# One transformer block on one core: the second sequence's value units moved up, and the shared opening in a new order

## The reference

```
xn = layernorm(x)
q, k, v, o = xn @ Wq.T, xn @ Wk.T, xn @ Wv.T, xn @ Wog.T
i, f = 15*tanh((xn @ Wig.T + big)/15), 15*tanh((xn @ Wfg.T + bfg)/15)
for each token t, each head:
    m' = max(logsigmoid(f) + m, i);  F = exp(logsigmoid(f) + m - m');  I = exp(i - m')
    C = F*C + I*k v^T;  n = F*n + I*k;  m = m'
    h = (q/sqrt(32)) C / (max(|q/sqrt(32) . n|, exp(-m)) + 1e-6)
x = x + (sigmoid(o) * gamma * headnorm(h)) @ Wout.T
w_q = sign(w) * (|w| >= 0.7 * mean|w|)            for w1 (2048x512) and w2 (512x2048)
x = x + gelu(layernorm(x) @ w1_q.T + b1) @ w2_q.T + b2
```

## Time and profile before

| | |
|---|---|
| median of three runs | 1740.55 us |
| the profiled execution, whole | 1742.3 us |
| its span (first to last instruction) | 1740.6 us |
| mean granted TensorE clock | 0.996 |
| busy: VectorE, ScalarE, POOL | 83%, 61%, 35% |
| instructions | 31380 |
| moved by DMA | 187.45 MB, mean 108 GB/s |

### The profile page before, as it was taken

One profiled execution on the slowest core, in us unless ns is written; L12 is line 12 of the kernel. 1 busy time (PEld: TensorE's weight loads), 2 busy tenths in 40 slices (PEclk: granted clock), 3 DMA queues, 4 the chain that ended last, 5 costly groups with the idle time before them and its releaser, 6 DMA issues.

```text
span 1740.6 us, 31380 instructions
## 1 busy us (share of the span) xinstructions
PE 1707.5 (98%) x12028; PEld 841.4 (48%) x12028; DVE 1437.6 (83%) x2528; ACT 1059.6 (61%) x1769; POOL 606.6 (35%) x477
## 2 busy tenths in 40 slices
PE   6899999999999999999999999999999999999999
PEld 4554445444444444445444444444444444454455
DVE  7888788897888978789887888988789788886872
ACT  6978375473746638375573746648375573847643
POOL 1242514335241442514235241442514235241430
PEclk9999999999999999999999999999999999999999
DMA  8736253442725326253442725336262442625120
GB/s 321 219 89 167 58 141 72 117 120 56 170 60 127 87 80 160 58 154 59 120 117 56 171 60 126 87 92 152 55 161 61 110 119 56 148 59 132 33 55 25
DMA packets 294981, 187.45 MB, mean 108 GB/s; under 512 B 239136, under 2 KB 260640, under 8 KB 289712
## 3 DMA queue, kind: packets, MB, share of 16 engines
q1 hardware_dynamic: 293248, 182.30, 41.7%
q10 hardware_dynamic: 1584, 3.15, 0.5%
HBM read 96.47 MB, written 20.23 MB: 67 GB/s over the span
## 4 chain that ended last, share of the span: by engine, by line
PE 81%; DVE 8%; DMA 3%; SPq 3%; issue 2%; POOL 1%; ACT 1%; POOLq 0%; DVEq 0%; ACTq 0%
PE pf L2073 24%; PE pf L2057 22%; PE pa L1926 17%; PE pa L1902 7%; PE psh L1926 5%; SPq L530 2%; PE psh L2013 2%; DMA kT<-shared 1%; PE psh L1968 1%; PE psh L2047 1%; DVE gT L1633 1%; PE pa L2013 1%; DVE dec L1482 1%; PE pa L1893 1%; PE psh L2009 1%
## 5 line engine op out<-in xcount | busy, mean ns | idle before, releaser
L2073 PE MATMUL pf<-w2T,gT 128*128 128x512 f16 x2048 | 505.8, 379 | 0.0
L2057 PE MATMUL pf<-x2T,w1T 128*128 128x512 f16 x1920 | 422.0, 379 | 0.0
L2057 PEld LDWEIGHTS pf<-x2T,w1T 128*128 128x128 f16 x1920 | 185.4, 98 | 222.5
L2073 PEld LDWEIGHTS pf<-w2T,gT 128*128 128x128 f16 x2048 | 195.5, 97 | 177.0
L1633 DVE SCALAR_TENSOR_TENSOR gT<-g,wscale,gT 128x512 f16<-128x512 f32 x240 | 208.5, 871 | 22.5 <-ACT gT L1046 20.2
L1926 PE MATMUL pa<-wT,xT 128*128 128x512 f16 x960 | 212.8, 379 | 0.6 <-ACT sig L970 0.6
L1043 ACT ACTIVATE g<-pf,b1c 128x512 f32<-128x512 f32 x240 | 164.1, 684 | 72.5 <-PE pf L2057 56.6
L1046 ACT ACTIVATE gT<-g,wscale 128x512 f16<-128x512 f32 x240 | 173.3, 722 | 7.9
L1926 PE MATMUL pa<-wT,shared 128*128 128x512 f16 x768 | 176.2, 379 | 1.6 <-DMA shared<-qT 0.8
L1051 ACT ACTIVATE ktok<-kT 128x512 f32<-128x512 f32 x64 | 40.4, 631 | 216.4 <-DVE kT L1528 214.9
L1902 PE MATMUL pa<-xT,wT 128*128 128x512 f16 x768 | 171.4, 379 | 0.0
(11 more groups left out here) (246 smaller groups left out, 2705.2 us busy)
## 6 DMA issues: line engine op xcount, KB each, us to landing
dec<-gate_r SPq DMA_DIRECT2D x32, 1024.0 KB, 6.1
xin<-L_attn_x SPq DMA_DIRECT2D x16, 1024.0 KB, 6.0
out<-x1b SPq DMA_DIRECT2D x64, 256.0 KB, 2.3
xres<-L_attn_x SPq DMA_DIRECT2D x16, 512.0 KB, 4.3
xres<-L_attn_x SPq DMA_DIRECT2D x32, 256.0 KB, 3.0
qw<-gate_w SPq DMA_DIRECT2D x128, 48.0 KB, 2.0
s<-state_w SPq DMA_DIRECT2D x60, 97.5 KB, 2.4
qw<-kT SPq DMA_DIRECT2D x120, 48.0 KB, 2.0
```

The source lines that it names most:

```text
L2057: last = nc.tensor.matmul(bank, w1T[:, k, tok(f)], x2T[:, part, :, k, :], start=(k == 0 and part == HI), stop=(k == KD - 1 and part == LO))
L2073: last = nc.tensor.matmul(bank, gT[:, part, f, tok(t)], w2T[:, f, :], start=(f == 0 and part == HI), stop=(f == NF - 1 and part == LO), sk ...
```

## The change

What moves, by engine:

- TensorE: the transpose of the row maxima and their sum are two functions, with x's transposes or weight transposes between them. gates(0), which put four slices of k side by side on column quarters, is first_gates, which sums all twelve matmuls on one set of 32 rows. scores(0, 1) stands ahead of the ternary transposes 2 to 4. Of the 18 filler matmuls ahead of ternary transpose 10, five stay; value unit 1 of sequence 1 follows them, in the bank pf[:, 1]. Value units 2 and 3 of sequence 1 stand ahead of project(0, 2).
- VectorE: no sum of gate quarters in sequence 0, and its gate logarithms stand in the setup; the high half of x(1) and the absolute sums of a quarter of w1 (absolute_sums) stand ahead of chunk_decay; the low half of x(1) stands between weigh(3) and weigh(4). The halves lie in xres and no longer in g32 and qT.
- ScalarE: the first function is a square of a small constant; tanh of sequence 0 reads the product directly; the sums of w1 and w2 are in another order, with two of w1 gone; squares of chunks 0 and 1 come ahead of a small2_gone each; value unit 1 of sequence 1 is copied out in the middle of the ternary work.
- POOL: in sequence 0 the masks wait for the decays' exponentials (d_ok), and weigh waits for the masks.
- SP: the order is the same; the load of xres for sequence 0 also waits for x(1)'s transposes.

The core of the diff:

```diff
-        x1_halves = [part[:, :, :].bitcast(F16).rearrange("p g s -> p (g s)").rearrange("p (t d) -> p t d", d=D) for part in (g32, qT)]
+        x1_halves = [part[:, :, :].bitcast(F16).rearrange("p g s -> p (g s)").rearrange("p (t d) -> p t d", d=D) for part in (xres[:, 0:T // 2, :], xres[:, T // 2:T, :])]
...
+                    sp.wait_ge(x1T_loaded, 32)
...
             def earlier_only(b, n):
-                for h in (2 * n, 2 * n + 1):
-                    if in_ps(h):
-                        pool.wait_ge(ps_free[h % 2], ps_done(b, h))
-                    else:
-                        pool.wait_ge(pa_free[h % 2], pa_done(b, score_use(h)))
+                if isinstance(b, int) and b == 0:
+                    pool.wait_ge(d_ok, 2 * n + 2)
+                else:
+                    for h in (2 * n, 2 * n + 1):
+                        if in_ps(h):
+                            pool.wait_ge(ps_free[h % 2], ps_done(b, h))
+                        else:
+                            pool.wait_ge(pa_free[h % 2], pa_done(b, score_use(h)))
...
-                value(b, 1)
+                if not (isinstance(b, int) and b == 1):
+                    value(b, 1)
...
+            def first_exponents():
+                bank = pa_bank(0, U_GATE)
+                act.wait_ge(pa_fill, pa_filled(0, U_GATE))
+                nc.scalar.activation(th, pa[0:GROWS, bank, :], ACT.Tanh, bias=gate_bias[:, 0:1],
+                                     scale=evac[0:GROWS, W_GATE:W_GATE + 1]).then_inc(tanh_ok, 1)
+                act.wait_ge(tanh_ok, 1)
+                nc.scalar.activation(ge, th[0:NH, :], ACT.Abs).then_inc(pa_free[bank], 1)
+                act.wait_ge(pa_free[bank], pa_done(0, U_GATE))
+                nc.scalar.activation(ge, ge, ACT.Exp, scale=-CAP).then_inc(gate_act, 1)
             def opening():
-                gate_copy(0)
-                absolute_sums2(1, 2)
-                gate_tanh(0)
+                absolute_sums2(0)
+                first_exponents()
+                absolute_sums2(1)
                 value(0, 0)
-                gate_exp(0)
-                absolute_sums1(6, early=True)
+                gate_log(0)
                 weights_hi(*USES_QK[0:3])
                 value(0, 1)
                 weights_hi(USES_QK[3])
-                gate_log(0)
+                replace_rows(G_QK)
+                absolute_sums1(6, early=True)
                 value(0, 2)
-                replace_rows(G_QK)
                 weights_hi(*USES_O[0:2])
+                gate_floor(0)
                 value(0, 3)
-                gate_floor(0)
                 act.wait_ge(s_abs, sums.n)
                 keys(0, 0)
                 late_decays(0)
                 weights_hi(USES_O[2])
                 keys(0, 1)
-                absolute_sums2(3)
                 weights_hi(USES_O[3])
+                absolute_sums2(2)
                 replace_rows(G_O)
                 queries(0, 0)
                 gate_columns(0)
-                absolute_sums1(7, 0)
+                absolute_sums2(3)
                 queries(0, 1)
-                absolute_sums1(1, 2, 3)
+                absolute_sums1(7, 0, 1)
                 output_gate(0, 0)
                 absolute_sums1(4)
                 output_gate(0, 1)
...
                 decay(0, 2)
                 output_gate(0, 3)
                 decay(0, 4)
+                decay(0, 6)
                 ternary_out(0)
-                decay(0, 6)
...
-                    bank, free = ps[:, 1, :], ps_free[1]
+                    bank, free = pf[:, 1, :] if isinstance(b, int) and b == 1 else ps[:, 1, :], ps_free[1]
...
                     ternary_out(5)
+                    squares(b, 0)
                     small2_gone(9)
                     ternary_out(6)
                     small2_gone(10)
-                    squares(b, 0)
                     ternary_out(7)
                     weights_hi(*USES_OUT[0:2])
+                squares(b, 1)
+                if not run_f:
                     small2_gone(11)
-                squares(b, 1)
                 gated_hi(b, 0)
                 if not run_f:
                     ternary_out(8)
                     small2_gone(12)
+                    ternary_out(9)
                 squares(b, 2)
                 if not run_f:
                     weights_hi(*USES_OUT[2:4])
                 gated_hi(b, 1)
                 if not run_f:
-                    ternary_out(9)
+                    value(1, 1)
                     small2_gone(13)
                     ternary_out(10)
...
+            act.wait_ge(s_pchain, 1)
+            nc.scalar.activation(hinv[:, :], half[:, :], ACT.Square).then_inc(s_table, 1)
             sum_squares(G_V)
             sum_squares(None)
-            sum_squares(G_QK)
             split_hi(*range(KD))
             weights_hi(*USES_V)
             weights_hi(USE_GATE)
             replace_rows(G_V)
-            absolute_sums2(0)
+            sum_squares(G_QK)
             sequence(0, None, True)
...
+            def absolute_sums(n):
+                dve.wait_ge(s_w12[0][n], 16)
+                nc.vector.tensor_reduce(asum1[:, 2 * n:2 * n + 2],
+                                        rows[:, 4 * n:4 * n + 4, :].rearrange("p (n u) d -> p n (u d)", u=2), AX.X, ALU.add,
+                                        apply_absolute_value=True).then_inc(s_abs_dve, 1)
             def thresholds():
-                dve.wait_ge(s_abs, 4 + UNITS // 2)
+                dve.wait_ge(s_abs, 4 + UNITS // 2 - 2)
+                dve.wait_ge(s_abs_dve, 1)
...
-            def split_x1():
+            def split_x1_hi():
                 dve.wait_ge(xn_ok, 2 * T)
+                dve.wait_ge(s_abs, ABS_RES)
                 nc.vector.tensor_scalar(x1_halves[HI], xin[:, :, :], X_SCALE, None, ALU.mult).then_inc(x1_hi, 1)
+            def split_x1_lo():
                 dve.wait_ge(x1_hi, 1)
-                dve.wait_ge(qw_ok, 1)
                 nc.vector.scalar_tensor_tensor(x1_halves[LO], xin[:, :, :], X_SCALE, x1_halves[HI],
                                                ALU.mult, ALU.subtract).then_inc(x1_ok, 1)
...
+            def first_floor():
+                dve.wait_ge(tanh_ok, 1)
+                nc.vector.tensor_scalar(gf, th[0:NH, :], CAP, 0.0, ALU.mult, ALU.min)
...
-                dve.wait_ge(d_ok, at(b, NH, n + 1))
+                if isinstance(b, int) and b == 0:
+                    dve.wait_ge(masked, n // 2 + 1)
+                else:
...
                     norm_apply(b + 1, range(T))
+                    split_x1_hi()
+                    absolute_sums(1)
                     chunk_decay(b)
                     thresholds()
                     small_gone(0, 1)
                     key_tokens(b)
                     small_gone(2, 3)
-                    split_x1()
...
                     if not run_f and n == H4:
+                        split_x1_lo()
                         small_gone(4)
...
+            row_maxima(1)
             bounds(EARLY, 1)
             split_lo(0, 1)
             scales(EARLY, 1)
             split_lo(2, 3)
-            weights_lo(*USES_V)
+            weights_lo(*USES_V[0:2])
             weights_lo(USE_GATE)
+            weights_lo(*USES_V[2:4])
             largest()
-            gate_sum(0)
+            first_floor()
+            row_maxima(2)
+            gate_one(0)
             bounds(LATER, 2)
+            gate_rest(0)
+            scales(LATER, 2)
+            weights_lo(*USES_QK)
             sequence(0, None, True)
...
+            def first_gates():
+                bank = take_pa(0, U_GATE)
+                for k in range(KD):
+                    for n, (ws, xs) in enumerate(PARTS):
+                        last = nc.tensor.matmul(bank[0:QUAD, :], wgT[:, k, ws, :], xT[:, xs, :, k, :],
+                                                start=(k == 0 and n == 0), stop=(k == KD - 1 and n == 2))
+                last.then_inc(pa_fill, 1)
...
-                    pe.wait_ge(masked, at(b, NH // 2, NH // 2))
-                    if not (isinstance(b, int) and b == 0):
+                    if isinstance(b, int) and b == 0:
+                        for n in (H4, H4 + 1):
+                            pe.wait_ge(ps_free[n % 2], ps_done(b, n))
...
                 if first:
                     opening()
-                else:
+                elif not (isinstance(b, int) and b == 1):
                     late_values(b, 2)
                     late_values(b, 3)
...
                 weights_ready(USE_GATE)
-                gates(0)
-                weights(*USES_QK[0:2])
+                first_gates()
                 weights_ready(*USES_V)
                 tokens(0, U_V, xT[:, :, 0, :, :], C_V)
-                maxima(3, 1, 2)
-                weights(USES_QK[2])
+                peak_transpose(3, 1, 2)
+                weights(USES_QK[0])
+                peak_sums(2)
+                weights(*USES_QK[1:3])
                 late_values(0, 1)
                 pe.wait_ge(s_bound, 2)
```

(18 more changed lines are left out.)

54 lines of the change are left out of this document (29 added, 25 removed).

## The result

The changed kernel takes 1746.97 us (median of 5 runs, 1745.87 to 1749.23) against 1740.55 (5 runs, 1740.49 to 1741.91): ratio 1.0038, 95% interval 1.0028 to 1.0049. It is 6.4 us slower, and I had forecast 1740.4 with a range to 1742.9. The profiled execution took 1745.87 with a span of 1744.1.

A forecast was written before the change was run, and what follows sets the result against it. TensorE, 98% busy, bounds the kernel; only its last late wait counts. E moves 0.3 later (g 1.0, w 0.3), less 0.5 room gives -0.2 us at scores(1,1): 1740.4 us, chance 0.60; range 1737.3 to 1742.9, chance 0.85.

The forecast's parts named there:

- first rival: Setup: input-gate rows land with their earlier issue, at 35 to 36; shift -2.5 us, 1738.0 us, chance 0.14.
- E: End of project(0,3) on TensorE, 118.60 us before; forecast 119.6 - g + w = 118.9, 0.3 later.
- second rival: Behind E: distances are not fixed, so the 4.9 us TensorE is ahead stay; 1735.7 us, chance 0.10.
- g: Sequence 0 up to its heads: gain taken as 1.0 us, bounds -1.5 and 3.
- w: Run to E: what is left of TensorE's waits, 0.3 us, 0 to 1 at the extremes.
- The masks now run on the decays, before weighing: Sequence 0: first head no longer waits for POOL's last mask, 1.8 us after the weighs; heads begin 1.5 early.
- Squares of chunk 1 and the small part swap places within ScalarE's slack: ScalarE in sequence 0: this reordering was given no cost.
- ScalarE's decays are 0.4 early: Sequence 0: ScalarE loses two sums of w1 (2.4 us), takes one of w2 (2.0), so decays come 0.4 early.
- The 20.8 us of work in the run to E: TensorE from 98.8 - g: four projections 10.4, ternary transposes 1.8, gates 0.8, unit 0 2.6, units 2 and 3 5.2.
- The third: Slower rival, sequence 0: VectorE's 3.5 us ahead of fcol delay the heads; shift 2.2, 1742.8 us, chance 0.16.
- shift: TensorE's change at scores(1,1) of sequence 1, 0.4 - g + w: -0.2 us, extremes -2.8 to +3.0.
- room: Slack in the distance from E to scores(1,1) of sequence 1: 0.5 us, range 0.35 to 0.8.

The follow-up runs named there:

- the moved copy: Copy of value (1,0) put ahead of sequence 1's gate exponential on ScalarE; alone on the kernel before 1740.28 us, with unit 1 early too 1740.43 us.
- the one with the value part alone: Kernel before with value unit 1 in place of 13 fillers and units 2 and 3 ahead of project(0,2): 1743.28 us, ratio 1.0018.
- everything priced put back: Changed kernel with masks, units 2 and 3, squares' order and x(1)'s high half put back, value (1,0) copied ahead of the gate exponential: 1742.43 us.

## Why the prediction was wrong

**Right.** The gate rows still land at 39 (39.14): first rival dead. The new gate products took 4.22 us (4.3 said), fcol came at 61.63 (61.6). The distance behind E is nearly fixed: scores(1,1) at E + 38.1, for 38.3 from the earlier trace rows; in the twelve other kernels without the moved copy and without a clock fall behind E it is E + 37.9 to E + 39.4, under 38.9 in ten of them. The second rival is dead with that. The wait of 3.2 us ahead of gate_columns(1) is there, in two pieces (1.83 and 1.26). By my own sign, scores(1,1) after 159, the forecast is wrong: 161.38.

**The step that failed is g, "the heads' gain", +1.0 by the text, bound -1.5.** By my own formula E = 119.6 - g + w, and the sum starts when VectorE's last Wout split ends: at 101.66 for 98.8. So g was -2.85, outside its lower bound, and E was 123.28. Its parts:

- "The masks now run on the decays, before weighing": I credited their going from the end of the path (POOL released the first head) and charged nothing where they came to. They cost 2.5 us of VectorE ahead of the weighs: weigh(0) at 71.82 where I said 69.0, weighs end at 80.85 for 78.2, first head 82.15 for 78.7. In time 2.3 us, by two runs, one in each direction.
- "Squares of chunk 1 and the small part swap places within ScalarE's slack", and I did not price the squares of chunk 0 at all. For the second there was no slack: alone on the kernel before it costs 3.0 us, the first up to 1. In the changed kernel with masks and units back, undoing both returned nothing. From the first head to project(0,0) it takes 19.9 us for 18.9; that this 1 us is held by the new order and by ScalarE's late sigmoid, each by itself, is read from two runs that removed one of them.
- "ScalarE's decays are 0.4 early" left out that two evictions now wait for transposes behind scores(0,1): 4.92 us idle to 78.21, sigmoid table at 80.16 for 75.04.

**w, "what is left of the waits"**, 0.3 said, was about 0.85 (0.38 ahead of project(0,0), 0.46 in the run from there to E), inside its bounds.

**The sum.** I set the moved units (5.2 in) against unit 1 (2.6 out) and 13 fillers. On the kernel before the in alone costs 4.7 and the out alone returns nothing, since its 2.6 us turn into waits for the gate sum and the value copy; together +3.0, part of it perhaps clock falls. The 20.8 us of work in the run to E were right: 21.26 measured, 0.46 of it waits, in the changed kernel and in the one with the value part alone. So the net of this part, 1.3 us on E, was nearly right (1.8), and the step that failed is not here. Of the three waits behind E (1.83, 1.26, 1.13) I had the first two as one. The first and the last are for banks that ScalarE frees behind the gate's last exponential. They cost nothing more by themselves, because they lie inside the nearly fixed distance; a clock fall behind them does.

**The rivals.** The third named the right mechanism, VectorE's and ScalarE's work ahead of the heads standing uncovered, and put its end at 1742.8, since g's lower bound was taken from single operations that could be dear, never from two engines slowing each other. What the sum then gives: shift = 0.4 + 2.85 + 0.85 = 4.1 us, measured 4.46 at scores(1,1). (The 0.4 should read 0.5: E's 119.6 less 118.6 less the room of 0.5. That makes it 4.2.) On the median 1744.6 would follow; the 2.3 us to 1746.97 are not in the profiled pair of executions. Part of that is settled: seven of the kernels above keep before's opening and masks, and in six of them the first head comes at 79.4 to 79.8 (80.15 in the seventh), not at 80.24, so the true shift is larger by about 0.6 and the profile I forecast from was a late one. The rest stays open; clock falls (below) could give part of it.

**Still open.** The 1.9 us with everything priced put back: 0.9 is seen as ScalarE's late sigmoid, up to 0.7 as unit 1 early, neither by a run of its own in that setting. Also open is how much of the median's 6.4 us clock falls are.

## What to carry to other kernels

Moving an instruction of an idle engine beside the work of another is not free where the two slow each other: look for the same pair side by side in the trace of before (here 2.24 us against 1.41) and price the move by it. In an engine that works in order, an instruction moved ahead charges its wait to everything it passed, so ask when its input comes, not how long it takes. And work taken out of a run counts only up to the next wait it was hiding: list the waits under it before you subtract.
